# A four-layer hybrid network on one core: work at odd units moved in front of VectorE's product, and four kinds of small VectorE work given to TensorE and ScalarE

## What is computed

```python
x = L0_conv(x)                       # expand to 576 channels, 5x5 depthwise, squeeze-excite, back to 96
x = x + L1_conv(group_norm(x))       # in-projection, 3x3 depthwise, selective scan over 4 directions, gate
t = t + L2_attn(layer_norm(t))       # a mixer: transform over the pixels, products per frequency, back
t = t + L2_ffn(layer_norm(t))        # feed-forward 96 -> 384 -> 96, fp8 products, fp16 sums
t = t + L3_attn(layer_norm(t))       # linear attention by a 97x97 Gram matrix
t = t + L3_ffn(layer_norm(t))

# the selective scan, for 768 channels (d) and 16 states (n) of a sample
dA = exp(dt * A);  h = dA * h + (dt * u) * B;  y = sum_n h * C

# the feed-forward (q_mul rounds to fp8 e5m2, q_acc to fp16)
y = q_acc(q_acc(q_mul(x) @ q_mul(W1)) + q_mul(b1));  h = relu(y)
y = q_acc(q_acc(q_mul(h) @ q_mul(W2)) + q_mul(b2))

# layer_norm over the 96 channels: (t - mean) / sqrt(mean((t - mean)^2) + eps)
```

## Time and profile before

| | |
|---|---|
| median of 3 runs | 26279.49 us |
| the profiled execution, its own time | 26389.19 us |
| its span | 26387.5 us |
| VectorE busy | 24513.9 us (93%) |
| TensorE busy | 20581.9 us (78%) |
| ScalarE busy | 11550.1 us (44%) |
| GpSimd busy | 8808.6 us (33%) |
| TensorE's granted clock, mean | 0.819 |

### The profile page before, as it was taken

How to read it: one execution, slowest core, us unless ns; L and a number is a source line. 1 busy time by engine, 2 the same in 40 slices (tenths; PEclk the granted TensorE clock), 3 DMA queues, 4 the chain that set the end, 5 groups by cost and what they waited for, 6 DMA issues and landing times.

```text
span 26387.5 us, 375604 instructions
## 1 busy us (share of the span) xinstructions
PE 20581.9 (78%) x125002; PEld 8812.8 (33%) x125002; DVE 24513.9 (93%) x23378; ACT 11550.1 (44%) x15421; POOL 8808.6 (33%) x4999
## 2 busy tenths in 40 slices
PE   6778778787787787877877878778778787787786
PEld 2333333333333333333333333333333333333332
DVE  5999999999999999999999999999999999999998
ACT  2444444444444444444444444444444444444443
POOL 2333333333333333333333333333333333333331
PEclk8878888888788888887888878888888788888886
DMA  2222222222222222222222222222222222222222
GB/s 74 66 71 67 68 72 62 72 69 64 71 67 68 71 62 72 69 64 71 67 67 72 62 71 70 64 71 67 67 72 62 71 69 65 71 67 67 72 62 61
DMA packets 646792, 1791.26 MB, mean 68 GB/s; under 512 B 76999, under 2 KB 87059, under 8 KB 644760
## 3 DMA queue, kind: packets, MB, share of 16 engines
q1 hardware_dynamic: 624280, 1726.94, 22.6%
q10 hardware_dynamic: 20480, 38.29, 0.5%
HBM read 1707.39 MB, written 44.96 MB: 66 GB/s over the span
## 4 chain that ended last, share of the span: by engine, by line
DVE 37%; issue 34%; PE 20%; ACT 5%; DVEq 2%; POOL 1%; DMA 0%; SPq 0%; ACTq 0%; POOLq 0%
DVE prod L1064 15%; PE bank L457 11%; DVE state L1233 9%; PE pair L457 6%; DVE drive L1064 5%; PE scan_sum L457 4%; DVE work L1064 2%; ACT work L825 1%; POOL drive L1467 1%; DVE delta L1064 1%; ACT decay L825 1%; ACT L825 1%; DVE work L1308 1%; DVE work L1332 1%; DVE pwm L1153 1%
## 5 line engine op out<-in xcount | busy, mean ns | idle before, releaser
L1467 POOL TENSOR_TENSOR drive<-du,Bb 128x784 f32<-128x784 f32 x3072 | 5964.3, 1941 | 14627.3 <-DVE drive L1064 14627.3
L457 PE MATMUL scan_sum<-prod,fold 64*64 64x392 f32 x40960 | 6452.5, 594 | 2647.4 <-DVE prod L1064 2644.8
L457 PE MATMUL bank<-pad,dg 64*64 64x392 f32 x59008 | 7515.6, 501 | 222.5 <-ACT pad L825 149.0
L825 ACT ACTIVATE decay_even<-delta,alog 128x784 f32<-128x784 f32 x3072 | 2817.9, 917 | 10807.9 <-DVE state L1233 10764.1
L1064 DVE TENSOR_TENSOR prod<-state,Cb 128x784 f32<-128x784 f32 x6144 | 6245.0, 1016 | 0.0
L1233 DVE TENSOR_TENSOR_SCAN state<-decay,drive 128x784 f32<-128x784 f32 x3072 | 5771.6, 1879 | 243.3 <-DVE pwm L1153 11.8
L1233 DVE TENSOR_TENSOR_SCAN state<-decay_even,drive 128x784 f32<-128x784 f32 x3072 | 5484.7, 1785 | 151.8 <-ACT decay_even L825 83.6
L457 PEld LDWEIGHTS bank<-pad,dg 64*64 64x64 f32 x59008 | 3410.3, 141 | 3883.7 <-issue 3103.2
L457 PEld LDWEIGHTS scan_sum<-prod,fold 64*64 64x64 f32 x40960 | 1746.3, 151 | 6143.1 <-issue 3819.4
L1064 DVE TENSOR_TENSOR drive<-du,Bb 128x784 f32<-128x784 f32 x3072 | 3006.6, 979 | 116.5 <-issue 116.5
L1410 POOL TENSOR_SCALAR_AFFINE_SELECT dg<-kern 128x640 f32<-128x640 f32 x1600 | 2542.7, 1593 | 1674.6 <-PE bank L457 1389.9
(11 more groups left out here) (176 smaller groups left out, 17363.3 us busy)
## 6 DMA issues: line engine op xcount, KB each, us to landing
Bb<-bc_rows SPq DMA_DIRECT2D x2048, 392.0 KB, 3.6
Cb<-bc_rows SPq DMA_DIRECT2D x2048, 392.0 KB, 4.2
xin<-in_x SPq DMA_DIRECT2D x64, 294.0 KB, 4.3
x_kept<-xin ACTq DMA_DIRECT2D x64, 294.0 KB, 4.6
x<-x_kept SPq DMA_DIRECT2D x64, 294.0 KB, 3.9
out_dram<-t SPq DMA_DIRECT2D x64, 294.0 KB, 2.7
crossed<-pwm ACTq DMA_DIRECT2D x128, 96.0 KB, 2.1
delta<-in_x SPq DMA_DIRECT2D x8, 1176.0 KB, 7.6
```

The source lines that it names most:

```text
L457: return pe.matmul(out, lhsT, rhs, start=start, stop=stop)
L825: return act.activation(out, in_, f, bias=bias, scale=scale, **more)
L1467: pool.tensor_tensor(drive[:, j % 2, :], du[:, m, :], Bb[:, q % SLOTS, :], ALU.mult).then_inc(drive_r.sem, 1)
```

## The change

It does five things.

1. `go_on(between, j)` stands in front of `driving(j + 1)` in odd units of VectorE.
2. `go_on` takes the generators' steps together, in the order of their positions, on every engine.
3. A layer norm's first matrix is `less96`, the unit matrix minus 1/96, so that TensorE's product is already centred. ScalarE copies it to `w[0]` and squares it to `w[1]`, both from PSUM. VectorE's subtraction goes.
4. The feed-forward's bias and relu, and its last bias, are ScalarE's, in place on the fp16 tile. VectorE keeps the casts and the sum. `xn1` is ScalarE's too.
5. `TAIL_AT` puts most steps of the tail about 3 units earlier.

```diff
-TAIL_AT = ((0, 9.8), (6, 20.0), (11, 24.8), (16, 29.6), (20, 39.5), (21, 41.0), (25, 47.5), (32, 53.5),
-           (40, 61.0), (48, 71.0), (56, 80.0), (62, 83.5), (70, 89.5), (78, 95.0))
+TAIL_AT = ((0, 9.8), (6, 17.0), (11, 21.8), (16, 26.8), (20, 36.8), (21, 38.3), (25, 44.5), (32, 50.5), (40, 58.0), (42, 60.0),
+           (48, 67.5), (51, 70.5), (60, 81.0), (62, 83.0), (70, 90.6), (78, 95.4))
...
-    for s in steps:
-        while s.at <= at:
-            s.next()
+    while steps and min(s.at for s in steps) <= at:
+        min(steps, key=lambda s: s.at).next()
...
-                    mm(T[h][0:C, 0:HALF], mean96[:, :], t2[:, h * HALF:(h + 1) * HALF]).then_inc(lm.sem, 1)
+                    mm(T[h][0:C, 0:HALF], less96[:, :], t2[:, h * HALF:(h + 1) * HALF]).then_inc(lm.sem, 1)
...
+                yield GATE_AT + 10.6
+                act.wait_ge(g_sh.sem, g_sh.at(i))
+                ac(xn1, xin[:, :], ACT.Identity, bias=gst[:, 7:8], scale=gst[:, 6:7]).then_inc(xn1_r.sem, 1)
...
-                yield tail_at(at + 2)
+                yield tail_at(at + 1.2)
...
-                    act.wait_ge(lc.sem, lc.at(i, 2 * n + h + 1))
-                    ac(w[1][0:C, cols[h]], w[0][0:C, cols[h]], ACT.Square).then_inc(lq.sem, 1)
+                    act.wait_ge(lm.sem, lm.at(i, 2 * n + h + 1))
+                    ac(w[0][0:C, cols[h]], T[h][0:C, 0:HALF], ACT.Copy)
+                    ac(w[1][0:C, cols[h]], T[h][0:C, 0:HALF], ACT.Square).then_inc(lq.sem, 1)
...
-                        ac(h16[:, m, h * HALF:(h + 1) * HALF], T[h][:, 0:HALF], ACT.Copy).then_inc(h_16.sem, 1)
+                        t = h16[:, m, h * HALF:(h + 1) * HALF]
+                        ac(t, T[h][:, 0:HALF], ACT.Copy).then_inc(h_16.sem, 1)
+                        act.wait_ge(h_16.sem, h_16.at(i, q))
+                        ac(t, t, ACT.Relu, bias=ffn_b1[f][:, m:m + 1]).then_inc(h_b.sem, 1)
...
+            v.tensor_scalar(less96[:, :], ident[0:C, 0:C], -1.0 / C, None, ALU.add)
...
-                v.tensor_scalar(xn1, xin[:, :], gst[:, 6:7], gst[:, 7:8], ALU.mult, ALU.add).then_inc(xn1_r.sem, 1)
...
                     if j >= 1:
                         product(j - 1)
+                    go_on(between, j)
                     if j % 2 == 1 and j + 1 < NU:
                         driving(j + 1)
-                    go_on(between, j)
...
-                    tt(w[0][0:C, cols], t2[:, cols], T[h][0:C, 0:HALF], ALU.subtract).then_inc(lc.sem, 1)
...
-                        v.tensor_scalar(t, t, ffn_b1[f][:, m:m + 1], 0.0, ALU.add, ALU.max).then_inc(h_b.sem, 1)
...
-                    link(v.tensor_scalar(o16[:, cols], o16[:, cols], ffn_b2[f][:, :], None, ALU.add))
```

More of the change, by code:

```diff
@@ L40 @@
 SETUP_LINKS = 53
-LEAD_LINKS = 14
-TAIL_LINKS = 6
+LEAD_LINKS = 13
+TAIL_LINKS = 2
 DVE_LINKS = LEAD_LINKS + TAIL_LINKS
@@ L157, in build @@
         mean96 = sb("mean96", [C, C])
+        less96 = sb("less96", [C, C])
         mean192 = sb("mean192", [128, 128])
@@ L280, in build @@
         x1_st, x1_in = sig("x1_stored", 16), sig("x1_loaded", 16)
-        g_in, g_mm, g_ve, g_rs, xn1_r = sig("group_stats"), sig("group_mm"), sig("group_var"), sig("group_rstd"), sig("xn1_ready")
+        g_in, g_mm, g_ve, g_rs, g_sh, xn1_r = sig("group_stats"), sig("group_mm"), sig("group_var"), sig("group_rstd"), sig("group_shift"), sig("xn1_ready")
         win_mm, p3_r, c3_mm, xc_r = sig("in_proj", 2), sig("conv_in", 2), sig("conv3_mm", 2), sig("conv_out", 2)
@@ L295, in build @@
         yg_r = sig("scaled192", S3)
-        lm, lc, lq, lv, ll, lr, ln_r = (sig("norm_mean", 8), sig("norm_centred", 8), sig("norm_squares", 8), sig("norm_var", 8),
+        lm, lq, lv, ll, lr, ln_r = (sig("norm_centred", 8), sig("norm_squares", 8), sig("norm_var", 8),
                                         sig("norm_log", 8), sig("norm_rstd", 8), sig("normed", 4))
@@ L301, in build @@
         h_mm, h_16, h_b, h_q = sig("ffn_up_mm", 12), sig("ffn_up_16", 12), sig("ffn_up_bias", 12), sig("ffn_up_8", 12)
-        o_mm, o_16, o_r = sig("ffn_down_mm", 4), sig("ffn_down_16", 4), sig("ffn_added", 4)
+        o_mm, o_16, o_b, o_r = sig("ffn_down_mm", 4), sig("ffn_down_16", 4), sig("ffn_down_bias", 4), sig("ffn_added", 4)
         tr_mm, tr_r = sig("tokens_mm", 2), sig("tokens_ready", 2)
@@ L1018, in ffn @@
                     act.wait_ge(o_mm.sem, o_mm.at(i, 2 * f + h + 1))
-                    ac(o16[:, h * HALF:(h + 1) * HALF], T[h][0:C, 0:HALF], ACT.Copy).then_inc(o_16.sem, 1)
+                    t = o16[:, h * HALF:(h + 1) * HALF]
+                    ac(t, T[h][0:C, 0:HALF], ACT.Copy).then_inc(o_16.sem, 1)
+                    act.wait_ge(o_16.sem, o_16.at(i, 2 * f + h + 1))
+                    ac(t, t, ACT.Identity, bias=ffn_b2[f][:, :]).then_inc(o_b.sem, 1)
             def attention(i):
@@ L1186, in pre @@
                 v.wait_ge(g_pw.sem, g_pw.at(i))
-                link(v.scalar_tensor_tensor(gst[:, 7:8], gst[:, 2:3], -1.0, gst[:, 6:7], ALU.mult, ALU.mult))
-                v.tensor_scalar(xn1, xin[:, :], gst[:, 6:7], gst[:, 7:8], ALU.mult, ALU.add).then_inc(xn1_r.sem, 1)
+                v.scalar_tensor_tensor(gst[:, 7:8], gst[:, 2:3], -1.0, gst[:, 6:7], ALU.mult, ALU.mult).then_inc(g_sh.sem, 1)
                 yield from steps(i, 0, 4, GATE_AT + 30.4, 1.0)
@@ L1264, in norm @@
             def norm(i, at, n, out, **more):
-                yield tail_at(at + 1)
-                for h in range(2):
-                    cols = slice(h * HALF, (h + 1) * HALF)
-                    v.wait_ge(lm.sem, lm.at(i, 2 * n + h + 1))
-                    tt(w[0][0:C, cols], t2[:, cols], T[h][0:C, 0:HALF], ALU.subtract).then_inc(lc.sem, 1)
                 yield tail_at(at + 5)
                 v.wait_ge(lr.sem, lr.at(i, 2 * n + 2))
-                v.wait_ge(lc.sem, lc.at(i, 2 * n + 2))
                 alone()
@@ L1338, in ffn @@
                     cols = slice(h * HALF, (h + 1) * HALF)
-                    v.wait_ge(o_16.sem, o_16.at(i, 2 * f + h + 1))
-                    link(v.tensor_scalar(o16[:, cols], o16[:, cols], ffn_b2[f][:, :], None, ALU.add))
+                    v.wait_ge(o_b.sem, o_b.at(i, 2 * f + h + 1))
                     tt(t2[:, cols], t2[:, cols], o16[:, cols], ALU.add).then_inc(o_r.sem, 1)
```

1 line of the change is left out of this document (removed).

## The result

| | before | after |
|---|---|---|
| median | 26276.87 us (4 runs) | 25925.78 us (4 runs, 25901.6 to 25943.69) |
| ratio, 95% interval | | 0.9868 (0.9856 to 0.988) |
| the profiled execution, its span | 26389.19, 26387.5 | 25920.02, 25918.3 |
| VectorE busy, instructions | 24513.9, 23378 | 23299.7, 21779 |
| ScalarE busy | 11550.1 | 12372.3 |

The kernel is 1.3% faster. I had forecast 4%, 25230 us, with a range that ended at 25680: the direction was right, the size and the range wrong.

A forecast was written before the change was run, and what follows sets the result against it. VectorE bounds the kernel, busy 93%. 11.5 + 11.9 - 1.7 - (3.3 + 2.4 + 1.8 + 0.4) + 2.0 + 0.9 = 16.7 us a pass, 1035 us in 62, plus 20: 25334 us profiled, 25230 median; range 24930 to 25550, widened to 25680.

The forecast's parts named there:

- What leaves VectorE: VectorE's feed-forward bias and relu, norms' subtractions, last biases and xn1 go to other engines: 11.5 us a pass saved.
- The holds: Odd units: VectorE instructions no longer held by GpSimd's drive, 11.9 us a pass saved, less 1.7 for drives beside even scans.
- The named waits: New VectorE waits a pass: 3.3 us at the first norm, 2.4 at the transform, 1.8 at unit 92's cast.
- the attention's 9.4: VectorE's waits for the attention's small products: 9.4 us a pass, 0.9 less than before, possibly 4 either way.
- 105 us: ScalarE's added work priced by the skill page, 0.63 us for 392 elements: the forecast would be about 105 us later.
- Small waits, 0.4: Units 53 to 57 and the gate of layer 1: small waits put at 0.4 us a pass.
- The median is 0.9958 of that execution: Whole kernel: the runs' median taken as 0.9958 of the profiled execution, turning 25334 us into 25230.
- the edges: First and last scans outside the loop, and the last tail: 20 us more saved.
- rival 1: ScalarE's relu up to 0.92 us, cast pairs late, TensorE's attention arrears grow: saving 8 us a pass, 25765 us; chance 0.18.
- Rival 4: GpSimd's drive late behind a diagonal group, odd scans wait: up to 23 us a pass, 26650 us, slower; chance 0.04.
- Rival 3: VectorE's holds stay, under GpSimd's diagonals: the 11.9 lost, saving 4.8 us a pass, 25960 us; chance 0.06.
- Rival 2: No new waits for VectorE, the lining up erring by a slot: saving 24.6 us a pass, 24740 us; chance 0.06.

The follow-up runs named there:

- e18: e13 with the moved work (biases, relu, norms' subtractions, normalized x1) back on VectorE, swap kept: 25666.18 us, 0.9756 of the kernel before.
- e6: Kernel before with the moved work alone; drive ahead of the step, old table, old merging: 25813.9 us, 0.9795 of before.
- e7: Kernel before with swap, new table and merged order, the work staying on VectorE: 26393.79 us, 1.002 of before.
- e13: Kernel after, old table outside the attention, mixer's relu one slot earlier, TensorE's transform parts one unit earlier, feed-forward norm's product one later: 24947.09 us, 0.9479 of before.
- e17: e13 with the swap undone, VectorE's drive ahead of the step again in odd units: 25313.39 us, 0.9624 of before.
- e9: Kernel after with old due times from the inverse transform on, except the attention; new ones up to the transform's relu: 25434.56 us, 0.9663 of before.
- e16: Kernel after with old due times for mixer and transform, new ones from the first feed-forward on: 25785.07 us, 0.9795 of before.
- e2: Kernel after with the swap undone, VectorE's drive ahead of the step in odd units: 26662.73 us, 1.0143 of before.

## Why the prediction was wrong, step by step

1. *"What leaves VectorE", 11.5 us a pass.* Right as a price: 11.7 where few waits are left (e18). In the order of before it gave 8.7 (e6), with the new table 6.4 (e7 against after). In both VectorE's waits grew, by 3.6 and 3.3 us a pass with the 1.8 in front of the casts taken off: the other engines' chains did not get shorter with VectorE's.
2. *The holds, 11.9 less 1.7.* Each duration fell as forecast, summed over the loop: `du` 4.4, casts 2.9, `t` 1.5, the transform's additions 2.1, the held fold 1.6, of which the other fold, now under a diagonal, takes back 0.5. But not all of it is time. In e13 against e17 the product, the odd scan and one addition take back 2.6 us, the sum of all durations falls by 8.3 all the same, neighbours overlap by 1.5 less, and the pass is 6.2 shorter. From before to after the overlap falls from 20.1 to 17.4 us a pass, with fewer instructions and more waits. Work and holds together lowered VectorE's busy time by 19.1 against the 19.9 of my sum: over-sized by 0.8. As a price for the change, this step held.
3. *The named waits: 3.3 + 2.4 + 1.8 and the attention's 9.4.* Measured 3.9, 3.7, 1.9 and 8.7. This method, laying the orders side by side, held. The 1.3 us at the transform are TensorE's speed: behind its wait for ScalarE the expansion takes 1.96 us where I took 1.5 and the sum behind it 1.58 where I took 0.8, and the second `cosm` part takes 3.30 in the mean, at a granted clock of 0.87, where the kernel before has 2.84 at 1.00. I took durations from a place where TensorE had not stood idle. ScalarE's relu of 0.62 us in place of 0.5 added tenths. By the figures of the Trainium skill (ScalarE: Activation LUTs, "Rules for kernel authors") 0.63 was the estimate, and the trace agrees with it. But even its 105 us are a small part of the miss.
4. *"Small waits, 0.4."* This is the step that failed. It was 8.8 us a pass, in units 40 to 63, where I wrote that most results are ready a unit ahead and did not lay the orders side by side. For 4.2 of the 8.8, in units 41 to 47, a row of my own profile spoke against it: in before, units 36 to 48 have TensorE busy for 41.38 of 42.06 us. Where TensorE has no slack, a step that reaches it later is late for all that stands behind it. The 4.4 at units 59 and 63 had no such sign: in units 48 to 64 TensorE was busy for 53.23 of 64.87 us. Only the orders side by side could have shown them, and not in full, since a part is the clock again: the pointwise product that `xin` waits for takes 7.84 us in the mean in the kernel after, its first 3.8 at a clock of 0.57, and 6.19 us at 0.99 in e9, where nobody waits for it. Had I counted those units as I counted 16, 26 and 92, the forecast would have been 25334 + 8.4 x 62 = 25855 by the profile.
5. *"The median is 0.9958 of that execution."* That was 104 us of the miss, and with the 6 between the profile after and its median 110. The profiled execution after is at its median (25920 and 25926). The gap belonged to the one execution before, and I carried it over as a ratio.

Together, against the 25230: 8.6 us of idle time and 0.8 of busy time a pass are 583 us, the last point 110, the edges 3: the 696 us of the miss. The 8.6 are the 8.4 of the fourth step, 1.9 of the named waits, less 0.7 in the attention and 1.0 of other idle time that went. The title of rival 1, "the waits take more", came true, its mechanism did not: I gave it 18% and a price, 25765, still 161 us short, but its condition was a relu near 0.92 us and arrears in the attention, and the relu took 0.62, only the casts of unit 92 out of six pairs wait, and the attention waits less than forecast. Rival 4's mechanism is there as well, at one place: a diagonal in front of GpSimd's drive costs scan 41 its 1.9 us. Rival 3's too, at the one fold (0.5 us a pass). Rival 2 is refuted.

What stays open: `xin`'s 3.1 us in unit 63 were tied to the feed-forwards' times (e9, e16), but which instruction of that chain (ScalarE's relus ahead of the scales, the crossed weights' transfer, TensorE's 8 us of pointwise product, or the low clock under it) sets it was not tried. Nor was it tried to keep TensorE's clock up across its waits.

## What to carry to other kernels

When the engine that bounds a kernel is made faster, the other engines' chains keep their length in microseconds while their deadlines, set in units of the fast engine's work, come sooner: lay the orders side by side through the whole pass, not only where the change puts new steps. Begin where another engine is busy nearly all the time, but do not stop there: half of the waits that I missed stood where TensorE was busy for 82%. Where TensorE waits several us before a step, price the step at the clock that the trace grants after such a wait. Try a table of due times apart from the work it was tuned with: here it cost half of what the rest gained (5.6 of 11.2 us a pass), and with a better one the same work and swap gave four times the gain of this change. Take the price of a held instruction from start to start, and set the profiled execution against the median before carrying a difference between them forward.

## What the runs showed of the hardware

- VectorE's scalar-tensor fold of 99x768 took 1480 ns in the kernel after, beside GpSimd's diagonal (1.50 us, started 0.8 us before it), and 946 in e13: diagonals hold VectorE as drives do.
- ScalarE's relu from fp16 in SBUF, 128x392, takes 622 ns, its copy from PSUM to fp16 some 480.
- TensorE's mean granted clock was 0.812 in e2, 0.819 before, 0.835 after, 0.848 in e13. It does not go by the time alone: e7 had 0.838 in 26387.7 us, before 0.819 in 26387.5. TensorE's work stayed the same, and its busy time in the windows of pass 31 fell from 320 us to 315 in e13.
- After a wait of 7.13 us TensorE worked at a granted clock of 0.50, and eight matmuls of the inverse transform behind it took up to 4.18 us in place of 2.90. A wait for another engine cost time a second time there.
